# Decoder layer on one core: the last two turns reordered, and the closing layer norm laid out 32 tokens in a row per partition

## The chip, the cores and the metric

One NeuronCore of a Trainium2 chip runs one program. Times are device microseconds (us) of that core. TensorE is called PE here, VectorE DVE, ScalarE ACT, GpSimd POOL and SyncE SP, as in the profile's rows.

## What is computed

A post-norm decoder layer on x of 16 sequences by 256 tokens by 512 features (N = 4096 tokens), all in float32:

```
x = _layernorm(x + _L0_attn_ref(x, ...))             # grouped-query attention, 16 heads of 32, rope
x = _layernorm(x + _L0_xattn_ref(x, ctx, ctx, ...))  # mLSTM: gated decay, per-head norm of h
x = _layernorm(x + _L0_ffn_ref(x, ...))              # top-2 of 16 experts + one shared expert
```

Inside the mLSTM each head's output is normed: `hn = (h - mu) * rsqrt(var + EPS)`. The feed-forward part routes each token to two of 16 experts (`silu(flat @ Wu[e]) * (flat @ Wg[e])) @ Wd[e]`) and adds a shared expert that all tokens pass.

## The kernel before, in words

The program has three blocks, one after the other, on all five engines.

**Turns** (`attention_and_mlstm`). The 16 sequences go through a software pipeline. A turn handles attention of sequence `b`, the mLSTM of `y = b - 1`, and router plus shared expert of `w = b - 2`. There are 18 turns; the last two are short: turn (None, 15, 14), in which no attention is left, and turn (None, None, 15), in which only routing and the shared expert of the last sequence are left. Each engine has its own instruction stream, written out by hand in `body` (SP, POOL, ACT, PE) and `front`/`back` (DVE); engines meet at semaphores (`sig`, `wait`). An engine runs its stream in order, so what stands behind a waiting instruction waits too.

The names that the change touches:

- `hvar`: 128 tokens by 2 x 16 heads, the variance of each head's output plus a floor. DVE writes it in `spread` (L909, L910, signal `hvar_done`). POOL takes it to the power -1/2 (L527, `hrstd_done`), and DVE multiplies the heads by it (L1065), then scales, adds and takes the second layer norm (L1067 to L1074), and writes `x2` (L1088, `x2_done`). PE's next turn starts with the transposes of `x2` (L1160).
- `down(t)`: the second matrix product of the shared expert (PE, L1414, two halves of 8 instructions each, signal `sd_ready`). DVE adds `x2` of the sequence before to it and gets `base` (L1079), before it overwrites `x2`.
- `ug(c)`: the first product of the shared expert, four chunks, each `su` (8 instructions) and then `sg` (8), L1205; ACT takes a tanh of it, and DVE makes `hT` from it in `hidden(c)` (L888, L893). `ug(c)` waits for `hidden(c - 2)`.
- `rank`: for the tokens of a sequence, the number of earlier tokens that chose each expert (PE, L1180 and L1181), from the one-hot choice that DVE makes (L959 to L971). DVE reads it (L767) and computes each token's row (`place_rows`), the shares, and in the last turn `first_tables` (L836 to L857), which ends with a small diagonal matrix.
- PE spreads that matrix over all partitions (L1249, `across_ready`), and DVE's `last_tables` (L863 to L882) makes the tables that steer the experts: `idx` first, then counts, slots and turns.
- With `idx` POOL fetches the first four lists of rows (`fetch_pairs`, L1448) and then gathers rows of `x2` (L1533).

**Experts** (`experts`). 79 tiles of 128 routed rows: PE transposes a gathered tile (L1647), multiplies (L1659), transposes (L1669) and multiplies again (L1678); POOL adds the scaled result to `sum_rows` in DRAM (L1548). PE starts this block once the last `base` is made.

**Finish** (`finish`). SP loads `sum_rows` in 8 groups of 1024 KB (L1733), DVE takes mean and variance (L1770, L1773), ACT applies them (L1748), and SP stores each group (L1736). Group g holds 4 tiles of 128 tokens; in a tile, partition p holds one token:

```
sum_v = sum_dram[0:N, :].rearrange("(t p) d -> p t d", p=P)
out_v = out.rearrange("b (t p) d -> p (b t) d", p=P)
```

So a partition's part of a group is four pieces of 2 KB from four places in DRAM.

## Time and profile before

| what | value |
|---|---|
| median of 3 runs | 2074.43 us (2070.18 to 2075.65) |
| the profiled execution, its own time | 2060.83 us |
| its span in the profile | 2059.3 us |
| granted clock of PE, mean over the span | 0.949 |
| busy share PE / DVE / ACT / POOL | 90% / 53% / 32% / 33% |
| start of turn (None, None, 15) on PE | 1497.7 us |
| start of the experts' first product | 1535.0 us |
| start of the finish block's loads | 2013.3 us |

The span is read from the first to the last instruction of the profiled execution; its own time lies 1.5 us above the span, and 13.6 us under the median of the three runs. Times in the rows below are from the start of the span. A timeline row gives start, duration, engine, line, operation, what is written and read, the count, and in brackets how long the engine sat idle before and what ended that. PEclk is the granted clock of PE: 1.00 is 2.4 GHz, 0.50 is 1.2 GHz.

### The profile page before, as it was taken

What the parts mean: (1) busy time and instruction counts of PE and PEld (TensorE: products, weight loads), DVE (VectorE), ACT (ScalarE), POOL (GpSimd) and SP (SyncE); (2) the same over time, 40 slices, a digit from 0 to 9 for tenths busy, and PEclk for the clock granted to TensorE, in tenths of its full rate; (3) what the DMA queues carried; (4) which work ended last, traced back from release to release, by engine and by line L of the source; (5) the groups of instructions that cost most, each with busy time, mean ns of one, the idle gap of its engine ahead of it and who ended that gap; (6) DMA issues with size and microseconds to landing.
All of it is one profiled execution on the core that took longest, in us unless ns stands there. A gap on an engine that the chain in (4) does not pass through costs nothing.

```text
span 2059.3 us, 35236 instructions
## 1 busy us (share of the span) xinstructions
PE 1847.0 (90%) x10928; PEld 1164.1 (57%) x10929; DVE 1101.3 (53%) x2408; ACT 649.0 (32%) x1371; POOL 689.3 (33%) x753
## 2 busy tenths in 40 slices
PE   5789999899999989899999989998779999999990
PEld 3457575666657566565756656575544444444440
DVE  3366675666667566666756666665442222222225
ACT  0243342424334252433424243332302212221224
POOL 3223233242322424132232423233133444444440
PEclk7889999999999999999999999999989999999995
DMA  5744244433524444242434334232324666656549
GB/s 159 206 87 110 69 94 106 96 101 61 120 65 97 112 90 105 56 120 63 99 94 106 99 65 120 62 80 67 110 97 99 128 168 164 151 120 146 90 74 336
DMA packets 151804, 225.94 MB, mean 110 GB/s; under 512 B 32272, under 2 KB 107024, under 8 KB 149200
## 3 DMA queue, kind: packets, MB, share of 16 engines
q1 hardware_dynamic: 101856, 132.41, 25.3%
q0 software_dynamic: 38112, 91.86, 19.8%
q10 hardware_dynamic: 11792, 1.13, 0.5%
q8 instruction: 22, 0.36, 0.1%
q14 instruction: 22, 0.18, 0.0%
HBM read 94.44 MB, written 48.57 MB: 69 GB/s over the span
## 4 chain that ended last, share of the span: by engine, by line
PE 77%; DVE 10%; issue 4%; ACT 3%; DMA 2%; another core or an unknown queue 1%; SPq 1%; POOL 1%; DVEq 0%; ACTq 0%; POOLq 0%
PE ps L1659 13%; PE ps L1205 10%; PE ps L1137 8%; PE ps L1678 7%; PE ps L1439 5%; PE ps L1414 5%; PE ps L1298 4%; PE ps L1403 4%; PE ps L1334 3%; PE ps L1281 3%; DVE smax L917 3%; DVE arden L935 2%; PE ps L1152 2%; PE ps L1383 2%; PE ps L1260 2%
## 5 line engine op out<-in xcount | busy, mean ns | idle before, releaser
L1659 PE MATMUL ps<-ug_w,rowsT 128*128 x632 | 289.2, 601 | 7.9 <-SPq L1508 4.5
L1659 PEld LDWEIGHTS ps<-ug_w,rowsT 128*128 128x128 f32 x632 | 121.3, 193 | 162.0 <-issue 162.0
L1548 POOL DMA_INDIRECT sum_rows<-y_sb,pairs x79 | 125.7, 1591 | 245.6 <-DVE y_sb L1626 126.9
L511 POOL DMA_INDIRECT routed_ids<-pair_w,pos_w x64 | 64.0, 999 | 428.0 <-DVE pair_w L813 413.4
L935 DVE RECIPROCAL arden<-ps 128x256 f32<-128x256 f32 x64 | 112.5, 1758 | 177.1 <-PE ps L1403 174.2
L1137 PE MATMUL ps<-wqkv_sb,xT_sb 128*128 128x256 f32 (+1 forms) x512 | 174.7, 495 | 5.9 <-DMA wqkv_sb<-in_wqkv 5.9
L1030 DVE SCALAR_TENSOR_TENSOR weighted<-ps,decay 128x384 f32<-128x384 f32 x256 | 140.4, 554 | 61.9 <-PE ps L1281 53.5
L917 DVE TENSOR_REDUCE smax<-ps 128x2 f32<-128x512 f32 x256 | 163.8, 682 | 15.3 <-PE ps L1334 15.3
L1614 DVE SCALAR_TENSOR_TENSOR silu<-tanh,ps 128x256 f32<-128x256 f32 x79 | 33.3, 421 | 249.5 <-ACT tanh L1569 249.5
L668 ACT ACTIVATE decay<-ps,g_col 128x256 f32<-128x256 f32 x256 | 121.3, 474 | 139.9 <-PE ps L1262 103.0
L689 ACT ACTIVATE probs<-ps 128x1024 f32<-128x1024 f32 x128 | 125.8, 1022 | 80.9 <-PE ps L1383 80.9
L1678 PE MATMUL ps<-d_w,hidT 128*128 x316 | 148.6, 593 | 0.1
L1569 ACT ACTIVATE tanh<-ps 128x256 f32<-128x256 f32 x79 | 30.3, 384 | 370.9 <-PE ps L1659 361.6
L1137 PEld LDWEIGHTS ps<-wqkv_sb,xT_sb 128*128 128x128 f32 x512 | 96.8, 192 | 86.9 <-issue 79.4
L1334 PE MATMUL ps<-k_stack,q_stack 96*128 96x256 f32 x512 | 113.8, 327 | 30.6 <-DMA q_stack<-qkT_hi 12.9
L575 ACT COPY hid_sq<-ps 128x320 f32<-128x320 f32 x32 | 13.6, 425 | 397.0 <-PE ps L1137 397.0
L527 POOL TENSOR_TENSOR hvar<-hvar,eps_half 128x32 f32<-128x32 f32 x16 | 87.4, 5465 | 149.7 <-DVE hvar L910 149.7
L1205 PE MATMUL ps<-x2T,su_sb 128*128 128x256 f32 x512 | 125.5, 389 | 3.8 <-DVE hT L893 3.8
L1205 PE MATMUL ps<-x2T,sg_sb 128*128 128x256 f32 x512 | 121.6, 380 | 0.0
L1383 PE MATMUL ps<-q_stack,k_stack 98*128 98x256 f32 x512 | 92.0, 322 | 32.1 <-ACT probs L689 19.1
L1439 PE MATMUL ps<-wo_sb,hid_sq 128*128 128x512 f32 x256 | 114.3, 600 | 5.5 <-DVE hid_sq L937 5.5
L1298 PE MATMUL ps<-weighted,ctx_sb 128*32 128x256 f32 (+1 forms) x1024 | 109.4, 335 | 6.0 <-issue 5.3
(258 smaller groups left out, 3585.2 us busy)
## 6 DMA issues: line engine op xcount, KB each, us to landing
q_stack<-qkT_hi SPq DMA_DIRECT2D x128, 128.0 KB, 5.0
mk_stack<-ctxT_hi SPq DMA_DIRECT2D x128, 128.0 KB
mq_stack<-qkT_hi SPq DMA_DIRECT2D x128, 128.0 KB, 2.5
ug_w<-in_expert_ug SPq DMA_DIRECT2D x16, 1024.0 KB, 5.6
xT_sb<-in_xT SPq DMA_DIRECT2D x16, 512.0 KB, 3.3
x_sb<-in_x POOLq DMA_DIRECT2D x16, 512.0 KB, 3.8
ctxT_sb<-in_ctxT POOLq DMA_DIRECT2D x16, 512.0 KB, 4.6
ctx_sb<-in_ctx_in POOLq DMA_DIRECT2D x16, 512.0 KB, 8.1
```

The lines of the kernel that those rows point to most:

```text
L689: nc.scalar.activation(probs[:, i % 4, :, :, :].rearrange("p j t s -> p (j t s)"), ps[:, 2 * (i % 2):2 * (i % 2) + 2, :].rearrange("p j n ...
L917: nc.vector.tensor_reduce(smax[:, k, :], ps[:, 3 + 4 * (k % 2), :].rearrange("p (t s) -> p t s", s=S), AX.X, ALU.max).then_inc(smax_done.s ...
L935: nc.vector.reciprocal(arden[:, :], ps[:, 6 + c % 2, cols]).then_inc(arden_done.sem, 1)
L1030: nc.vector.scalar_tensor_tensor(weighted[:, h % 4, :], ps[:, qk2_bank(h), 0:384], SCALE, decay[:, h % 2, :], ALU.mult, ALU.mult).then_inc ...
L1137: ins = nc.tensor.matmul(ps[:, 2 * t + lo // 512, 0:hi - lo], xT_sb[:, c, P * t:P * t + P], wqkv_sb[:, c, lo:hi], start=c == 0, stop=c == ...
L1205: ins = nc.tensor.matmul(ps[:, 6 + c % 2, lo:lo + S], wt[:, k, P * c:P * c + P], x2T[:, k, :], start=k == 0, stop=k == KC - 1)
L1298: nc.tensor.matmul(ps[lo:lo + HD, 4 + i // 4, col + cols.start:col + cols.stop], ctx_sb[:, t, h, :], weighted[:, h % 4, part], start=t == ...
L1334: ins = nc.tensor.matmul(ps[:, 3 + 4 * (k % 2), S * t:S * t + S], q_stack[0:96, k, P * t:P * t + P], k_stack[0:96, k // GQ, :], start=True ...
L1383: ins = nc.tensor.matmul(ps[:, 2 * (i % 2) + j, S * t:S * t + S], k_stack[0:98, h // GQ, P * t:P * t + P], q_stack[0:98, h, :], start=True ...
L1439: ins = nc.tensor.matmul(ps[:, 6 + t, :], attT[:, c, P * t:P * t + P], wo_sb[:, c, :], start=c == 0, stop=c == KC - 1)
L1659: ins = nc.tensor.matmul(ps[:, 2 + k % 2, :], rowsT[:, k % 2, c, :], ug_w[:, bass.ds(slot, 1), c, :].rearrange("p o n -> p (o n)"), start= ...
L1678: ins = nc.tensor.matmul(ps[:, 4 + k % 2, :], hidT[:, k % 2, f, :], d_w[:, bass.ds(slot, 1), f, :].rearrange("p o d -> p (o d)"), start=f ...
```

## The change

Five edits; the first four act in the last two turns alone.

1. In turn (None, 15, 14) the power -1/2 on POOL is replaced by a square root on ACT (behind `square`) and a reciprocal on DVE. All other turns keep POOL's.
2. In the same turn both halves of `down` also wait for `hvar_done`.
3. In the last turn `rank` stands between the `su` and the `sg` half of `ug(0)`, not behind `ug(0)`, and the spreading of the diagonal matrix stands ahead of `ug(3)`, not behind it.
4. In the last turn `last_tables` stands ahead of `hidden(2)`, not behind `hidden(3)`.
5. In `finish`, partition p holds tokens 32p to 32p + 31, so that its part of a group is one piece of 8 KB, in `sum_rows` and in the output alike.

A signal is renamed too (`ln1_step` to `norm_step`), as the reciprocal steps it once more at the end.

```
                 if y is not None:
-                    wait(pool, hvar_done, y, 1)
-                    nc.gpsimd.tensor_tensor(hvar[:, :], hvar[:, :], eps_half[:, :], ALU.pow).then_inc(hrstd_done.sem, 1)
+                    if b is not None:
+                        wait(pool, hvar_done, y, 1)
+                        nc.gpsimd.tensor_tensor(hvar[:, :], hvar[:, :], eps_half[:, :], ALU.pow).then_inc(hrstd_done.sem, 1)
...
                         square()
+                        wait(act, hvar_done, y, 1)
+                        nc.scalar.activation(hvar[:, :], hvar[:, :], ACT.Sqrt).then_inc(hrstd_done.sem, 1)
...
                         nc.vector.tensor_tensor(g_log, g_cumf, g_max, ALU.add).then_inc(g_cols.sem, 1)
+                    if last:
+                        last_tables()
                     if w is not None:
                         hidden(2)
...
                         hidden(3)
-                    if last:
-                        last_tables()
...
                         wait(dve, hrstd_done, y, 1)
+                        if b is None:
+                            nc.vector.reciprocal(hvar[:, :], hvar[:, :]).then_inc(norm_step.sem, 1)
+                            wait(dve, norm_step, y + 1, 1)
                         wait(dve, hid_done, y, 2)
...
                             ins = nc.tensor.matmul(ps[:, 6 + c % 2, lo:lo + S], wt[:, k, P * c:P * c + P], x2T[:, k, :],
                                                    start=k == 0, stop=k == KC - 1)
+                        if c == 0 and lo == 0 and b is None and y is None:
+                            rank(ps[:, 0, 0:2 * ST * E])
...
-                    if b is None and y is None:
-                        rank(ps[:, 0, 0:2 * ST * E])
                     for c in range(1, SC):
                         if y is not None and c == 2:
                             rank(ranks_of_turn)
+                        if c == SC - 1 and b is None and y is None:
+                            pe.wait_ge(diag_done.sem, 3)
+                            nc.tensor.matmul(ps[:, 1, 0:3 * P], ones_k[:, 0:1].to_broadcast([P, P]), sq_flat[:, 0:3 * P],
+                                             start=True, stop=True).then_inc(across_ready.sem, 1)
                         ug(c)
-                    if b is None and y is None:
-                        pe.wait_ge(diag_done.sem, 3)
-                        nc.tensor.matmul(ps[:, 1, 0:3 * P], ones_k[:, 0:1].to_broadcast([P, P]), sq_flat[:, 0:3 * P],
-                                         start=True, stop=True).then_inc(across_ready.sem, 1)
...
                     elif y is not None:
                         wait(pe, decay_done, y, H)
+                        wait(pe, hvar_done, y, 1)
...
-        sum_v = sum_dram[0:N, :].rearrange("(t p) d -> p t d", p=P)
-        out_v = out.rearrange("b (t p) d -> p (b t) d", p=P)
+        sum_v = sum_dram[0:N, :].rearrange("(p t) d -> p t d", p=P)
+        out_v = out.rearrange("b s d -> (b s) d").rearrange("(p t) d -> p t d", p=P)
```

PE in the last turn, before (after the routing product L1173; `su_sb` and `sg_sb` are the two halves of `ug`, L1180 and L1181 the ranks, L1249 the spreading, L1414 `down`):

```order
L1205 MATMUL ps<-x2T,su_sb 128x256 x4
L1205 MATMUL ps<-x2T,sg_sb 128x256 x4
L1180 MATMUL ps<-biased,before_sb 128x32
L1181 MATMUL ps<-biased,ones_k 128x32
L1205 MATMUL ps<-x2T,su_sb 128x256 x4
L1205 MATMUL ps<-x2T,sg_sb 128x256 x4
L1205 MATMUL ps<-x2T,su_sb 128x256 x4
L1205 MATMUL ps<-x2T,sg_sb 128x256 x4
L1205 MATMUL ps<-x2T,su_sb 128x256 x4
L1205 MATMUL ps<-x2T,sg_sb 128x256 x4
L1249 MATMUL ps<-hid_sq,ones_k 128x384
L1414 MATMUL ps<-sd_sb,hT 128x512 x8
```

The same place in the changed kernel (its lines stand a few numbers later):

```order
L1211 MATMUL ps<-x2T,su_sb 128x256 x4
L1186 MATMUL ps<-biased,before_sb 128x32
L1187 MATMUL ps<-biased,ones_k 128x32
L1211 MATMUL ps<-x2T,sg_sb 128x256 x4
L1211 MATMUL ps<-x2T,su_sb 128x256 x4
L1211 MATMUL ps<-x2T,sg_sb 128x256 x4
L1211 MATMUL ps<-x2T,su_sb 128x256 x4
L1211 MATMUL ps<-x2T,sg_sb 128x256 x4
L1254 MATMUL ps<-hid_sq,ones_k 128x384
L1211 MATMUL ps<-x2T,su_sb 128x256 x4
L1211 MATMUL ps<-x2T,sg_sb 128x256 x4
L1421 MATMUL ps<-sd_sb,hT 128x512 x8
```

The ranks moved up by one half of `ug(0)`, the spreading by all of `ug(3)`; the count of instructions is the same. (The order's listing counts a float32 matmul once; the profile shows it as two.)

ACT at the end of turn (None, 15, 14) and the start of the last, in the changed kernel (L640 copies the heads' output, L645 is `square`, L590 and L600 belong to the last turn, L583 is its first tanh):

```order
L640 COPY hid_sq<-ps 128x2x256 [waits x2_done,num_ready]
L645 ACTIVATE weighted<-hid_sq 128x1024 [waits av2_pair,hid_done]
L686 ACT_TABLE_LOAD
L686 ACTIVATE hvar<-hvar 128x32 [waits hvar_done]
L590 COPY x2T<-ps 128x1024 [waits num_ready,x2T_ready]
L600 COPY arden<-ps 128x256 [waits lgT_ready]
L583 ACT_TABLE_LOAD [waits silu_done]
L583 ACTIVATE gate_sb<-ps 128x256 [waits ug_ready]
```

The two table loads and the square root (L686) are new; the load of L686 waits for no signal, and the square root waits for `hvar_done`.

## Rows read from the trace of the kernel before

**Rows 1.** The page, section 4: shares of the chain that ended last, by engine.
```profile
PE 77%; DVE 10%; issue 4%; ACT 3%; DMA 2%; another core or an unknown queue 1%; SPq 1%; POOL 1%; DVEq 0%; ACTq 0%; POOLq 0%
```
**Rows 2.** Timeline, DVE, end of turn (None, 15, 14).
```profile
1484.00 0.19 DVE L910 SCALAR_TENSOR_TENSOR hvar<-hvar,mrden 128x32 f32<-128x32 f32 x1
1489.78 1.22 DVE L1065 TENSOR_TENSOR hid_sq<-hid_sq,hvar 128x1024 f32<-128x1024 f32 x1 [5.59 <-POOL hvar L527]
...
1494.97 1.27 DVE L1079 TENSOR_TENSOR base<-ps,x 128x512 f32<-128x512 f32 x2
1496.38 1.22 DVE L1088 TENSOR_SCALAR x<-hid_sq,mv,rstd 128x512 f32<-128x512 f32 x2
```
**Rows 3.** Timeline, PE, same stretch.
```profile
1480.06 0.44 PE L1319 MATMUL ps<-id_sb,denT 128*128 128x128 f32 x2 [2.32 <-ACT denT L679]
...
1480.77 7.03 PE L1414 MATMUL ps<-sd_sb,hT 128*128 128x512 f32 x16
1497.66 1.97 PE L1160 MATMUL ps<-id_sb,x 128*128 128x128 f32 x8 [9.85 <-DVE x L1088]
```
**Rows 4.** Timeline, ACT, an earlier table load and the square of this turn.
```profile
1443.43 1.28 ACT L609 ACT_TABLE_LOAD   x1
...
1481.59 1.06 ACT L644 ACTIVATE weighted<-hid_sq 128x1024 f32<-128x1024 f32 x1
```
**Rows 5.** Windows: start:end, length, busy us of PE, PEld, DVE, ACT, POOL, PEclk, DMA share, GB/s.
```profile
1445.90:1447.80 1.90, 0.00 (x0) 0.00 (x0) 0.84 (x3) 1.28 (x3) 0.00 (x0) 1.00 0.93 195
1448.60:1452.00 3.40, 3.40 (x9) 2.66 (x8) 2.49 (x6) 0.00 (x0) 0.00 (x0) 0.50 0.00 0
...
1493.00:1506.50 13.50, 7.25 (x28) 5.35 (x29) 6.31 (x21) 1.38 (x2) 2.54 (x4) 0.50 0.57 228
```
**Rows 6.** Timeline, DVE, the last turn.
```profile
1503.37 0.19 DVE L959 COPY logits<-ps 128x32 f32<-128x32 f32 x1 [5.77 <-PE ps L1173]
...
1505.34 0.19 DVE L971 TENSOR_TENSOR biased<-onehot 128x32 f32<-128x32 f32 x1
1508.96 0.22 DVE L767 COPY hid_sq<-ps 128x64 f32<-128x64 f32 x1 [3.43 <-PE ps L1181]
...
1516.19 0.78 DVE L857 TENSOR_SCALAR hid_sq<-id_sb,hid_sq 128x128 f32<-128x128 f32 x3
...
1522.78 0.55 DVE L863 COPY hid_sq<-ps 128x384 f32<-128x384 f32 x1
...
1525.56 0.19 DVE L882 TENSOR_SCALAR turns<-hid_sq 1x79 int32<-1x79 f32 x1
...
1530.09 0.69 DVE L1079 TENSOR_TENSOR base<-ps,x 128x512 f32<-128x512 f32 x1 [2.74 <-issue]
```
**Rows 7.** Timeline, PE, the last turn and the experts' first tile.
```profile
1512.34 1.99 PE L1205 MATMUL ps<-x2T,su_sb 128*128 128x256 f32 x8
...
1521.37 0.81 PE L1249 MATMUL ps<-hid_sq,ones_k 128*128 128x384 f32 x2
1522.92 7.13 PE L1414 MATMUL ps<-sd_sb,hT 128*128 128x512 f32 x16 [0.74 <-DVE hT L893]
1532.50 0.63 PE L1647 MATMUL ps<-id_sb,rows 128*128 128x128 f32 x4 [2.44 <-DMA rows<-x_rows,pairs]
1535.00 6.53 PE L1659 MATMUL ps<-ug_w,rowsT 128*128 x8 [1.87 <-issue]
```
**Rows 8.** Time to landing of the loads L1733 and the stores L1736.
```profile
DMA to landing us min/median/max: 5.7/12.9/14.8
...
DMA to landing us min/median/max: 5.3/8.3/12.2
```
**Rows 9.** Landing of the expert weights' loads L1503; windows with 8 KB and with 2 KB pieces.
```profile
DMA to landing us min/median/max: 5.1/5.6/9.8
...
1488.00:1492.90 4.90, 0.00 (x0) 0.00 (x0) 3.05 (x3) 0.00 (x0) 1.74 (x1) 1.00 1.00 417
2016.00:2053.00 37.00, 0.00 (x0) 0.00 (x0) 26.27 (x88) 23.67 (x40) 0.00 (x0) 0.50 1.04 395
```

More of the change, by code:

```diff
@@ L281, in attention_and_mlstm @@
         wo_ready, h_done = sig("wo_ready", ST), sig("h_done", ST)
-        ln1_step, mv1_done, rstd1_step, rstd1_done = sig("ln1_step", ST), sig("mv1_done", ST), sig("rstd1_step", 1), sig("rstd1_done", 1)
+        norm_step, mv1_done, rstd1_step, rstd1_done = sig("norm_step", ST), sig("mv1_done", ST), sig("rstd1_step", 1), sig("rstd1_done", 1)
         x1_done = sig("x1_done", ST)
@@ L1096, in back @@
                             wait(dve, h_done, b, t + 1)
-                            nc.vector.bn_stats(stats1[:, t, :], x1[:, t, :]).then_inc(ln1_step.sem, 1)
+                            nc.vector.bn_stats(stats1[:, t, :], x1[:, t, :]).then_inc(norm_step.sem, 1)
                         for t in range(ST):
-                            wait(dve, ln1_step, b, t + 1, rest=rest)
+                            wait(dve, norm_step, b, t + 1, rest=rest)
                             nc.vector.bn_aggr(mv1[:, t, :], stats1[:, t, :]).then_inc(mv1_done.sem, 1)
```

## The prediction

> **What bounds the kernel now.** I first read the chain of waits: 77% of it is PE, 10% DVE [rows 1]. In the sixteen full turns and in the experts PE is nearly always busy, and the change leaves both alone. It works where PE is not the bound: from the end of turn (None, 15, 14) to the experts' first product, and in the finish block. So I took the timelines of DVE, PE and ACT there, then windows for PE's granted clock, then the DMA of the finish.
>
> End of turn (None, 15, 14): DVE has the variance at 1484.19, then sits idle for 5.59 us behind POOL's power, and writes x2 from 1496.38 to 1497.60 [rows 2]. PE has done both halves of down long before (1480.77 to 1487.80) and idles 9.85 us [rows 3]. This chain alone sets the start of the last turn.
>
> Last turn: let T be the start of the logits' copy, 1503.37. The choice is made at T + 2.2, but the ranks are read at T + 5.6, since they stand behind both halves of ug(0) on PE. The diagonal matrix is done at T + 13.6, 8.0 after the ranks; the tables are begun at T + 19.4 and take 3.0; the last base is made at T + 27.4 [rows 6]. PE begins the last down at T + 19.55, ends it at T + 26.7, and the first gathered rows come at T + 29.1, 1.7 after the last base; the first expert product starts at T + 31.6 [rows 6, 7].
>
> PE's clock: granted 0.50 from 1493.0 to 1506.5, after PE had done nothing since 1487.8 [rows 3, 5]. The experts' first product takes 6.53 us for 8 instructions [rows 7], where half as much is usual at the full clock.
>
> Finish: 16 transfers of 1024 KB are 16.8 MB. From 2016 to 2053 the DMA engines are busy all the time and move 395 GB/s [rows 9], and the last store lands 5.3 us after its issue [rows 8].
>
> **The root (edit 1).** Off the path: 5.59 us of DVE's idle time [rows 2]. On it come a square root on ACT and a reciprocal on DVE, 128 by 32 each. Neither is in the trace at this shape; the lower bound is DVE's 0.19 for the same shape [rows 2], the upper ACT's 1.06 for 32 times the elements [rows 4]. I take 0.2 each, the shape being the same, plus 0.2 for the hand-overs: 0.6. The table load costs 1.28 us [rows 4]; it waits for no signal, so it starts behind the square, at 1482.65, and is over at 1483.93, 0.26 before the variance. The load back for the tanh lies behind the copy of the logits' parts, where ACT waits for PE's ug(0): nothing. If that cover were gone it would be 1.28. So DVE's chain is **5.0 sooner** up to the norm's statistics, from about 1495.0 to 1490.0.
>
> **down held back (edit 2).** PE now starts down at about 1484.3, not 1480.8. At the full clock its 7.03 us end at 1491.3. The second half of base, which started at about 1495.6, needs that end plus 0.2; base and x2 follow, and x2 starts at 1492.3, so of the 5.0 only 4.1 are left. Moreover PE now does nothing from 1477.7 to 1484.3 except 0.7 us of transposes [rows 3]. The trace shows what less than that did: PE idle for 1.9 us ahead of 1447.8, and then 3.4 us at half the clock [rows 5]. In 3.4 us at half clock PE does 1.7 us of work less, so down ends at 1493.0 and x2 comes **2.4 sooner**. That is my value; bounds are 4.1 (no such stretch) and 0.7 (a stretch twice as long).
>
> **The clock after it.** Before, the first 13.5 us of the stretch from 1493.0 on have 7.25 us of PE work at half clock [rows 5], 3.6 at full; some 2 of the difference lie on the way to T. In the changed kernel PE's hole ahead of x2 shrinks from 9.85 to about 2 us, so the clock may stay up, but as the 1.9 us hole shows it need not. Between 0 and 2, I take **0.5**, near the lower end, since there the nearest row is the 1.9 us one.
>
> **Ranks and tables sooner (edits 3 and 4).** From T at full clock: choice at T + 2.2, ranks (0.8 with hand-over) read at T + 3.0, sg done at T + 4.9, diagonal matrix at T + 11.0. PE does ug(1) and ug(2), each 2 halves of 1.8 to 2.0 [rows 7], until T + 12.2, then the spreading (0.8) until T + 13.0. DVE's tables take 3.0, until T + 16.0; hidden(2) and hidden(3), now behind them, need 0.9 each and 0.4 for the tanh between: down starts at T + 18.2, not 19.55. The rows to be gathered are asked for some 6 us sooner and are no longer waited for; PE now goes on with the last base, T + 26.1, and needs about 2.6 from there (transposes, ACT's issue of two DMAs ahead of its copy, and the 1.87 of loads of registers [rows 7]): first product at T + 28.7 in place of 31.6. I take **2.8**; bounds 1.3 (only down's start moves) and 3.5.
>
> **The first product's clock.** PE's pause ahead of it falls from 2.44 + 1.87 to about 0.9 + 1.9. If the clock stays up, 6.53 becomes 3.3 [rows 7]. Between 0 and 3.2; I take **0.5**, as a pause of nearly 2 us remains.
>
> **Long rows in the finish (edit 5).** The nearest stretch with 8 KB pieces is the expert weights', with 4 KB ones among them: 417 GB/s at a DMA share of 1.00 [rows 9]. 16.8 MB take 42.5 us at 395 and 40.2 at 417: 2.2 less. But DVE and ACT need their own 30 us between first landing and last store; by the ends alone the first load could land at 5.1 instead of 5.7 and the last store at 5.1 instead of 5.3 [rows 8, 9], 0.8 in all. I take **1.6** between these two. Issue on SP is hidden behind DVE.
>
> The Trainium skill speaks against this part: its page "DMA: Bandwidth & Descriptors", section Specifications, has pieces of 512 B and more at line rate, so that 2 KB would be as good as 8 KB. By that rule the sum would be 1.6 smaller. The trace has 395 against 417 GB/s, so I keep my value.
>
> **Sum.** 2.4 + 0.5 + 2.8 + 0.5 + 1.6 = 7.8 us. The profiled execution took 2060.8, so I expect 2053.0 for it; against the median of the runs, 13.6 us higher, **2066.6**. About 0.3%, 6.2 us, is what a measurement of this kernel can tell from no change: the border is 2068.2.
>
> **Rivals.**
> - **The clock stays up.** PE's holes are all about 2 us or less but one, and several holes of that kind in the turns cost nothing. Then x2 gains 4.1, the way to T 2.0, the last turn 2.8, the first product 2.8, the finish 2.2: 13.9, 2060.5. Against it: the stretch after 1447.8 [rows 5].
> - **The held down gives back what the root gave.** Half clock lasts through nearly all of down; x2 gains 0.7, PE idles at the same places as before, the finish gives 0.8: with 2.8 for the tables 4.3, 2070.1. For it: the hole of 6.6 us with 0.7 of work in it is much longer than the 1.9 us that sufficed. Against it: down itself is 7 us of unbroken work, and 1448.6 to 1452.0 was short.
> - **Rows do not matter in the finish**, all else as forecast: 6.2, 2068.2, just on the border, counted as the same.
> - **The finish becomes slower.** All 128 partitions now read and write at a distance of 64 KB from one another, where a group was one closed piece of 1 MB. The turns and tables give 6.2, so the kernel is slower by 0.3% if the finish loses 12.4: 42.5 us become 55, at about 305 GB/s. If it ran at the 228 GB/s of [rows 5], as one example of a slow stretch, it would take 74 us, 31 more: 2099. Nothing in the trace shows such a pattern; the weights with 8 KB pieces lie close together.
>
> The Trainium skill knows such an effect, in the same page, section "Latency and other measured facts": distances between partitions' rows that are large powers of two slow the copies, but at 512 KiB it still has nearly the full rate. 64 KB is far below; no run here shows it yet.
>
> **Chances.** Forecast 0.52 (its own range 2063.5 to 2069.5, seven eighths of it under the border), clock stays up 0.15, given back 0.20, rows do not matter 0.08, slower finish 0.05. Faster by over 0.3%: 0.52 x 7/8 + 0.15 = 0.61. Slower 0.05, the rest, 0.34, the same. The range reaches from the second case to a little over the third: 2060 to 2072.
>
> **What would show it.** In the changed profile DVE's idle time ahead of the product with hvar falls to about 0.6; ACT shows a table load that ends before the variance; down starts at the variance. Whether PEclk is 0.50 within down decides between 2.4 and 4.1. T lies about 3 us sooner; ranks are read 3.0 after T; the experts' first transposes no longer wait for the gathered rows. In the finish the rate is above 410 GB/s, or the last part is wrong. I am wrong on the whole if x2 isn't sooner, or if the finish takes longer from its first load to the end than 46 us.

## The result, and the profile after

| | before | changed |
|---|---|---|
| median | 2074.61 us (22 runs, 2068.14 to 2077.86) | 2065.86 us (22 runs, 2056.83 to 2076.89) |
| the profiled execution, its own time | 2060.83 us | 2056.83 us |
| its span | 2059.3 us | 2055.3 us |
| granted clock of PE, mean | 0.949 | 0.951 |

The ratio of the times is 0.9962, 95% interval 0.9952 to 0.9972: 7.9 us faster (5.8 to 10.0), by more than the 0.3% that I called measurable, though the interval reaches a little below it. The medians themselves are 8.75 us apart. The forecast was 7.8 us less than the earlier median of three runs, 2066.6. One execution of the kernel before in the first batch of the experiments below took 3065 us at a mean clock of 0.554, and the ratios leave it out.

The two profiled executions differ by only 4.0 us. Both are unusually fast: the one before (2060.83) lies below the lowest of its 22 runs, and the changed one is the lowest of its own. The page shows nothing of where the difference comes from: the chain is PE 77% before [rows 1], and now

```profile
PE 78%; DVE 10%; ACT 4%; issue 3%; another core or an unknown queue 2%; DMA 1%; SPq 1%; DVEq 0%; ACTq 0%; POOLq 0%
```

So I cut each trace at places that both kernels have: the variance (end of L910, now L913), the start of x2 (L1088, now L1094), the logits' copy T (L959, now L962), the start of the first expert product (L1659, now L1666), its end, and the first load of the finish. Lengths in us:

| stage | before | changed |
|---|---|---|
| start of the span to the variance | 1484.2 | 1492.5 |
| variance to the start of x2 | 12.19 | 10.30 |
| x2 to T | 6.99 | 5.25 |
| T to the first expert product | 31.63 | 27.53 |
| that product (8 instructions) | 6.53 | 3.70 |
| its end to the finish's first load | 471.8 | 471.7 |
| finish, from its first load's issue to the end | 46.0 | 44.2 |

The last six are 12.3 us shorter. The first is 8.35 longer, in the sixteen full turns and the start, whose code is the same in both; that is how much executions of one program differ, and why a stage, not a span, is compared below. In the same way 12.3 is not the gain of a typical execution, as the experiments will show.

**The root.** DVE and ACT at the variance, changed kernel (timeline; compare [rows 2, 4]):

```profile
1491.01 1.28 ACT L686 ACT_TABLE_LOAD   x1
...
1492.35 0.19 DVE L913 SCALAR_TENSOR_TENSOR hvar<-hvar,mrden 128x32 f32<-128x32 f32 x1
1492.57 0.23 ACT L686 ACTIVATE hvar<-hvar 128x32 f32<-128x32 f32 x1 [0.28 <-DVE hvar L913]
1492.68 9.29 PE L1421 MATMUL ps<-sd_sb,hT 128*128 128x512 f32 x16 [3.78 <-DVE hvar L913]
1492.83 0.35 DVE L1068 RECIPROCAL hvar<-hvar 128x32 f32<-128x32 f32 x1 [0.29 <-ACT hvar L686]
1493.22 1.23 DVE L1071 TENSOR_TENSOR hid_sq<-hid_sq,hvar 128x1024 f32<-128x1024 f32 x1
```

The table load ends 0.28 us before the root starts, the root takes 0.23 and the reciprocal 0.35. From the variance's end (1492.54) to the product with hvar there are 0.68 us, where there were 5.59.

**down held back.** DVE gets the halves of down late (changed kernel, timeline), and the clock is half in a part of them (windows; columns as in [rows 5]):

```profile
1498.58 0.69 DVE L1085 TENSOR_TENSOR base<-ps,x 128x512 f32<-128x512 f32 x1
...
1502.01 0.69 DVE L1085 TENSOR_TENSOR base<-ps,x 128x512 f32<-128x512 f32 x1 [2.74 <-PE ps L1421]
1502.84 1.22 DVE L1094 TENSOR_SCALAR x<-hid_sq,mv,rstd 128x512 f32<-128x512 f32 x2
```
```profile
1488.90:1492.60 3.70, 0.01 (x1) 0.00 (x0) 1.89 (x5) 2.96 (x4) 0.00 (x0) 0.68 0.64 184
1492.60:1496.80 4.20, 4.12 (x5) 1.83 (x6) 3.87 (x4) 0.20 (x1) 0.00 (x0) 0.50 1.08 422
1496.80:1502.00 5.20, 5.17 (x12) 1.91 (x10) 2.36 (x6) 0.00 (x0) 0.95 (x2) 0.97 0.95 394
1502.00:1504.00 2.00, 0.00 (x0) 0.00 (x0) 1.85 (x3) 0.00 (x0) 0.83 (x1) 1.00 1.03 422
1504.00:1509.00 5.00, 3.30 (x25) 2.48 (x26) 0.86 (x7) 2.67 (x3) 0.76 (x1) 1.00 0.94 381
```

PE idles from 1488.9, its granted clock is 0.68 on average over that idle stretch and 0.50 in the first 4.2 us of down; down takes 9.29 us, not 7.03. DVE waits 2.74 us for it. In exchange the hole (PE's idle stretch) ahead of x2 is short, about 2.1 us, and the last turn begins at the full clock, where before it was half until 1506.5 [rows 5].

**Ranks and tables** (changed kernel, timeline of DVE, then of PE; compare [rows 6, 7]). T is 1508.09:

```profile
1508.09 0.19 DVE L962 COPY logits<-ps 128x32 f32<-128x32 f32 x1 [4.04 <-PE ps L1179]
...
1510.97 0.23 DVE L770 COPY hid_sq<-ps 128x64 f32<-128x64 f32 x1 [0.72 <-PE ps L1187]
...
1518.20 0.68 DVE L860 TENSOR_SCALAR hid_sq<-id_sb,hid_sq 128x128 f32<-128x128 f32 x3
...
1520.34 0.56 DVE L866 COPY hid_sq<-ps 128x384 f32<-128x384 f32 x1 [0.67 <-issue]
...
1522.82 0.19 DVE L885 TENSOR_SCALAR turns<-hid_sq 1x79 int32<-1x79 f32 x1
...
1532.31 0.69 DVE L1085 TENSOR_TENSOR base<-ps,x 128x512 f32<-128x512 f32 x1 [2.74 <-PE ps L1421]
```
```profile
1519.49 0.81 PE L1254 MATMUL ps<-hid_sq,ones_k 128*128 128x384 f32 x2
...
1525.13 7.13 PE L1421 MATMUL ps<-sd_sb,hT 128*128 128x512 f32 x16 [1.38 <-DVE hT L896]
1533.10 0.63 PE L1654 MATMUL ps<-id_sb,rows 128*128 128x128 f32 x4 [0.83 <-DVE base L1085]
1535.62 3.69 PE L1666 MATMUL ps<-ug_w,rowsT 128*128 x8 [1.90 <-ACT rowsT L1589]
```

Ranks are read at T + 2.9, the diagonal matrix is done at T + 10.8, the tables at T + 14.9, down starts at T + 17.0, the last base ends at T + 24.9, and the transposes follow base and no longer the gathered rows.

**Finish** (changed kernel: SP's issues, landing of the loads and of the stores, one window; compare [rows 8, 9]):

```profile
2011.04 4.04 SPq L1740 DMA_DIRECT2D ctotal<-sum_rows  x8
2025.69 25.04 SPq L1743 DMA_DIRECT2D out_rows<-ctotal  x8
```
```profile
DMA to landing us min/median/max: 4.8/11.8/20.6
...
DMA to landing us min/median/max: 4.5/7.8/12.0
```
```profile
2013.70:2050.70 37.00, 0.00 (x0) 0.00 (x0) 26.28 (x88) 24.19 (x40) 0.00 (x0) 0.50 1.00 411
```

411 GB/s in place of 395. SP issued the eight loads in 4.04 us; in the kernel before it took

```profile
2013.29 12.84 SPq L1733 DMA_DIRECT2D ctotal<-sum_rows  x8
```

The gain of the finish lies at its two ends. DVE's first instruction stands 4.8 us behind the first load's issue (before: 5.7), and the end of the kernel 4.9 us behind the last store's issue (before: 5.7). The time from the one to the other is 34.5 us in the changed kernel and 34.6 in the kernel before. In it DVE and ACT go from group to group, and DVE waits for a load only once, for the first. A few microseconds ahead of the last store's issue the DMA engines are still busy all the time in the kernel before, while in the changed kernel their share falls to 0.83 for 2 us (windows, the kernel before first):

```profile
2049.30:2053.30 4.00, 0.00 (x0) 0.00 (x0) 0.00 (x0) 4.00 (x7) 0.00 (x0) 0.50 1.05 408
```
```profile
2047.00:2049.00 2.00, 0.00 (x0) 0.00 (x0) 0.00 (x0) 2.00 (x4) 0.00 (x0) 0.50 0.83 348
```

### The profile page after: what moved, and what is told of

It reads as the page before. It is cut to its first block, busy times and chain, and to the rows that moved or that the text cites. A ratio compares the mean times of both kernels' runs of the same rounds, so it can differ in the third digit from the quotient of the medians.

```text
span 2055.3 us, 35239 instructions
## 1 busy us (share of the span) xinstructions
PE 1843.0 (90%) x10928; PEld 1163.2 (57%) x10929; DVE 1101.7 (54%) x2409; ACT 651.7 (32%) x1374; POOL 684.6 (33%) x752
## 4 chain that ended last, share of the span: by engine, by line
PE 78%; DVE 10%; ACT 4%; issue 3%; another core or an unknown queue 2%; DMA 1%; SPq 1%; DVEq 0%; ACTq 0%; POOLq 0%
PE ps L1666 13%; PE ps L1211 11%; PE ps L1143 8%; PE ps L1685 7%; PE ps L1421 6%; PE ps L1446 5%; PE ps L1409 4%; PE ps L1304 4%; PE ps L1340 3%; PE ps L1287 3%; DVE arden L938 3%; DVE smax L920 3%; PE ps L1158 2%; PE ps L1266 2%
## 5 line engine op out<-in xcount | busy, mean ns | idle before, releaser
L1666 PE MATMUL ps<-ug_w,rowsT 128*128 x632 | 286.3, 596 | 8.0 <-SPq L1515 4.6
L1666 PEld LDWEIGHTS ps<-ug_w,rowsT 128*128 128x128 f32 x632 | 120.2, 191 | 160.3 <-issue 160.2
L528 POOL TENSOR_TENSOR hvar<-hvar,eps_half 128x32 f32<-128x32 f32 x15 | 82.0, 5468 | 157.4 <-DVE hvar L913 157.4
L1421 PE MATMUL ps<-sd_sb,hT 128*128 128x512 f32 x256 | 116.3, 608 | 5.2 <-DVE hvar L913 3.8
```

The lines of the kernel that those rows point to most:

```text
L1421: ins = nc.tensor.matmul(ps[:, 2 + t, :], hT[:, c, P * t:P * t + P], sd_sb[:, c, :], start=c == 0, stop=c == SC - 1)
L1666: ins = nc.tensor.matmul(ps[:, 2 + k % 2, :], rowsT[:, k % 2, c, :], ug_w[:, bass.ds(slot, 1), c, :].rearrange("p o n -> p (o n)"), start= ...
```

## The experiments

The eleven runs came in three batches, on three chips. There the kernel before takes 1997 us (medians 1996.92, 1997.78 and 1997.26), where it took 2075 above; the record doesn't name the chip of the first pair, and I take it to be another. Nearly all of the difference lies ahead of the variance (1416 to 1423 us in place of 1484 and 1493). The stages behind it are about as long as above, but the stretch from the first expert product's end to the finish's first load, 471.8 and 471.7 us above, ranges from 471.4 to 474.2 us in the eleven profiles. The half-held version below has 474.0 in one execution and 471.4 in another, so even this stage moves by more than some of the gains looked for. Ratios are against the kernel before in the same batch. At the end of the section one table has the stages of all of them.

### Down not held back

```
-                        wait(pe, hvar_done, y, 1)
```

> The changed kernel without edit 2: both halves of down run again right behind the transposes, under the root. Theory (the hold costs what it takes from the root): from the variance to the start of x2 7.2 us, where the changed kernel's profile has 10.3 and the kernel before 12.2; PE then idles some 5 us ahead of x2 and its clock may fall there, so that from x2 to the logits' copy it is 5.3 to 7.0. In all 1 to 3 us faster than the changed kernel, ratio to the kernel before 0.9945 to 0.9957. Rival (the hold pays, because it keeps the clock up for the last turn): the half clock behind x2 takes 3 us or more, and the kernel is slower than the changed one, 0.9965 or above.

1987.23 us, ratio 0.9947 (0.9932 to 0.9961). x2 starts 7.29 after the variance, where 7.2 was expected, and then the way to T is 6.98. The ratio is within the range of the theory. All of the root's gain reaches x2, and PE has its hole again (timeline, PE; windows):

```profile
1429.18 1.11 PE L1166 MATMUL ps<-id_sb,x 128*128 128x128 f32 x4 [4.95 <-DVE x L1094]
```
```profile
1424.20:1429.00 4.80, 0.04 (x1) 0.00 (x0) 4.63 (x9) 0.00 (x0) 1.78 (x3) 0.76 1.02 369
1429.00:1431.00 2.00, 1.82 (x8) 1.57 (x8) 0.13 (x1) 0.00 (x0) 0.76 (x1) 0.50 0.97 401
1431.00:1434.90 3.90, 2.31 (x14) 1.28 (x14) 0.00 (x1) 2.50 (x3) 0.00 (x0) 0.50 1.02 426
1434.90:1439.90 5.00, 5.00 (x14) 4.17 (x15) 2.52 (x17) 0.17 (x1) 0.00 (x0) 0.50 0.52 211
```

The clock falls in the hole and is half for the 10.9 us from 1429.0 to 1439.9. So the two orders place one slow stretch differently: ahead of x2, or behind it.

### Pieces of 2 KB in the finish, as before

```
-        sum_v = sum_dram[0:N, :].rearrange("(p t) d -> p t d", p=P)
-        out_v = out.rearrange("b s d -> (b s) d").rearrange("(p t) d -> p t d", p=P)
+        sum_v = sum_dram[0:N, :].rearrange("(t p) d -> p t d", p=P)
+        out_v = out.rearrange("b (t p) d -> p (b t) d", p=P)
```

> The changed kernel without edit 5: four pieces of 2 KB per partition and group again. Theory (long rows move more bytes a second): the finish, from its first load's issue to the end, takes 46.0 us as before and not 44.3, first load landing 5.7 and last store 5.3 where the changed kernel has 4.8 and 4.5; ratio 0.997. Rival (the finish was sooner by chance, or because it began in a quieter moment): 44.3 us and 0.9962 again.

1991.4 us, 0.9973 (0.996 to 0.9986). The finish is 45.92 us again, with all else changed; its loads land after 5.6/12.9/14.9 us and the rate is

```profile
1950.00:1985.00 35.00, 0.00 (x0) 0.00 (x0) 26.26 (x88) 24.19 (x40) 0.00 (x0) 0.50 1.05 398
```

By the finish's length the long pieces are worth 1.7 us. That is edit 5 by itself, as forecast: the finish takes 45.6 to 46.0 us in the three profiles with 2 KB pieces and 43.8 to 44.6 in the ten with 8 KB. The ratio alone couldn't tell it (0.9973 here, 0.9965 and 0.9962 for the changed kernel, with overlapping intervals). Edit 5 changes two things at once, the length of a piece and the distance between the partitions' rows, and no run separates them. The code from the variance to the experts is here the changed kernel's word for word, and yet that way took 51.4 us up to the end of the first product, not 46.8: x2 to T 5.88, T to the product 29.22, the product itself 6.76. The clock goes with it. It is still 1.00 over the hole of 2.1 us ahead of x2's transposes, then 0.77 up to 1436.9, 0.54 in the 5.1 us after that, and 0.54 again in the product, where the changed kernel's profile has 1.00 in all of them.

### Ranks and tables late, as before

Edits 3 and 4 undone, all else changed:

```
-                        if c == 0 and lo == 0 and b is None and y is None:
-                            rank(ps[:, 0, 0:2 * ST * E])
...
+                    if b is None and y is None:
+                        rank(ps[:, 0, 0:2 * ST * E])
                     for c in range(1, SC):
...
-                    if last:
-                        last_tables()
                     if w is not None:
                         hidden(2)
...
                         hidden(3)
+                    if last:
+                        last_tables()
```

> The changed kernel without edits 3 and 4: ranks behind ug(0), spreading behind ug(3), last tables behind hidden(3). Theory: from the logits' copy to the experts' first product 31 to 31.6 us as before, where the changed kernel has 27.5; 4 us slower than the changed kernel, and up to 3 more where PE's clock falls in the longer pause ahead of the first product; ratio 0.9980 to 0.9995. Rival (down's start alone moved, the rest is the clock's): 28.8 us and less than 2 us slower.

1992.71 us, 0.9974 (0.9959 to 0.9989), under the 0.9980 to 0.9995 that was expected. Down starts 20.4 after T, the first product 32.5, and PE waits for the gathered rows again:

```profile
1465.91 0.63 PE L1654 MATMUL ps<-id_sb,rows 128*128 128x128 f32 x4 [2.33 <-DMA rows<-x_rows,pairs]
```

That is 4.9 more than 27.53, but here the clock was half for 5 us after T (0.50). Against the two profiles with the new order and the clock down in the same place (29.22 and 29.43) it is 3.0 to 3.3 more. By the ratio, edits 3 and 4 are worth about 2 us (0.9974 against 0.9965), which is not clear of the noise.

### The root on POOL, down not held

Edits 1 and 2 undone:

```
-                        wait(pe, hvar_done, y, 1)
...
-                        nc.scalar.activation(hvar[:, :], hvar[:, :], ACT.Sqrt).then_inc(hrstd_done.sem, 1)
...
-                            nc.vector.reciprocal(hvar[:, :], hvar[:, :]).then_inc(norm_step.sem, 1)
...
+                    wait(pool, hvar_done, y, 1)
+                    nc.gpsimd.tensor_tensor(hvar[:, :], hvar[:, :], eps_half[:, :], ALU.pow).then_inc(hrstd_done.sem, 1)
```

> The changed kernel without edits 1 and 2 (POOL's power again, down at once): tables sooner and long rows alone. Theory (edits 1 and 2 together are worth 2 to 4 us): from the variance to x2 12.2 us, to the logits' copy another 7.0 at half clock; ratio 0.9970 to 0.9985. Rival (the root with the hold is worth nothing over all executions): 0.9962.

1991.96 us, 0.9975 (0.9964 to 0.9985). DVE waits again:

```profile
1423.74 1.22 DVE L1065 TENSOR_TENSOR hid_sq<-hid_sq,hvar 128x1024 f32<-128x1024 f32 x1 [5.58 <-POOL hvar L527]
```

x2 starts 12.19 after the variance, and T to the product is 29.66: with the root as before, the earlier tables alone bring 2.0 of the 31.63. Against the first experiment, which differs from this one by the root alone, x2 is 4.90 later, and the time 4.7 longer (1991.96 and 1987.23; by the means of 10 and 5 executions 4.9, give or take 2.8). So the root's gain is seen in the stage and in the time alike.

### The changed kernel again, on one of these chips

No edit.

> The changed kernel itself, on the chip of the four runs before. Of the four parts each undone run bounds one: without edit 5 it had 0.9973, without edits 3 and 4 0.9974, with the held down taken back 0.9947. Theory (the held down costs more than it brings): 0.9955 to 0.9965 here, so slower than with down not held; x2 starts 10.3 us after the variance against 7.3, the way from the variance to the end of the first expert product is 47 to 52 us depending on whether PE's clock falls in the last turn. Rival (the held down pays by the clock after it): ratio 0.9940 or less, and the way to the first product's end is under 49.1, the value with down not held.

1990.06 us, 0.9965 (0.9949 to 0.9981). The profiled execution was one with the clock up in the last turn: T to the product 27.53, the product 3.70, to the hundredth as in the first profile; x2 starts 9.81 after the variance, not 10.30. So its stages speak for the rival, as they are shorter than with down not held (46.3 against 49.1 from the variance to the product's end), and its ratio for the theory (0.9965 against 0.9947, intervals overlapping). Both together, below, settles it.

### Only the second half of down held, until the product with hvar is made

```
                         wait(pe, decay_done, y, H)
-                        wait(pe, hvar_done, y, 1)
+                        if t == 1:
+                            wait(pe, tail_step, y, 5)
```

> The changed kernel, but the first half of down starts at once, and the second half waits until DVE has made the product with the reciprocal. Theory: PE's one hole ahead of x2 is then cut in two, of about 2 and 3 us, x2 starts as early after the variance as with down not held (7.3 us), and the last turn starts with the clock up in more executions: from x2 to the logits' copy 5.3 to 6 us instead of 7.0. Ratio 0.9935 to 0.9947. Rival (the clock falls with two holes of this size as with one): 7.3 and 7.0 us as with down not held, ratio 0.9947.

1984.97 us, 0.9933 (0.9918 to 0.9949). Timeline of PE, and windows:

```profile
1417.31 3.60 PE L1422 MATMUL ps<-sd_sb,hT 128*128 128x512 f32 x8
...
1422.78 3.67 PE L1422 MATMUL ps<-sd_sb,hT 128*128 128x512 f32 x8 [1.87 <-DVE hid_sq L1071]
...
1429.28 1.09 PE L1166 MATMUL ps<-id_sb,x 128*128 128x128 f32 x8 [2.83 <-DVE x L1094]
```
```profile
1426.50:1429.20 2.70, 0.00 (x0) 0.00 (x0) 2.56 (x6) 0.00 (x0) 1.78 (x3) 1.00 1.00 350
1429.20:1434.00 4.80, 3.12 (x21) 2.01 (x21) 0.03 (x1) 2.37 (x3) 0.76 (x1) 0.65 1.01 398
1434.00:1440.00 6.00, 6.00 (x23) 5.05 (x23) 3.59 (x23) 0.45 (x2) 0.00 (x0) 0.71 0.74 306
```

x2 is as early as with down not held, neither half of down is slowed, and the clock falls later and for less: 6.11 from x2 to T, in place of 6.98 (5.3 to 6 was expected). One hole of 4.95 has become two of 1.87 and 2.83. Of this kernel and the changed one in the same batch the medians are 5.1 us apart.

### Other ends of the finish

The first load in two halves, each with a signal of its own; the last group normalised by DVE itself. Two waits of SP that cost no time are added for the halves.

```
+            sp.dma_start(total[:, 0:G // 2, :], sum_v[:, 0:G // 2, :]).then_inc(out_sem, 16)
+            sp.dma_start(total[:, G // 2:G, :], sum_v[:, G // 2:G, :]).then_inc(total_in[0], 16)
...
+            dve.wait_ge(shift_done, NT // G)
+            for n in range(NT - G, NT):
+                v.tensor_scalar(total[:, n, :], total[:, n, :], rstd[:, n:n + 1], shift[:, n:n + 1],
+                                ALU.mult, ALU.add).then_inc(own_step, 1)
```

> The changed kernel with other ends of the finish: the first load is cut in two halves with a signal each, and DVE normalises the last group itself. With the DMA at its rate all the time, the finish is 16.8 MB at about 411 GB/s, 40.9 us, plus the first load's flight and the last store's. Theory (rows and ends set the finish, the middle is at the DMA's rate): 44.2 becomes 41.5 to 43 us, ratio 0.001 lower than the changed kernel's in the same batch. Rival (the middle absorbs it: the last load's landing sets the last store, not the first landing): under 0.5 us, no difference in the ratio.

1990.43 us, 0.9964 (0.995 to 0.9977), against 0.9965 for the changed kernel: nothing. From the first load's issue the finish takes 43.8 us, where it took 44.2; the other profiles with 8 KB pieces have 43.9 to 44.6, so this is no clear gain either. The theory fell. The rival was right in size but not in its reason, since the last store is issued much sooner: DVE begins 3.9 us after the first issue, in place of 4.8, and the last store is issued 36.3 us after it (1982.8 - 1946.5), in place of 39.2 (1981.5 - 1942.3). But from there it takes 7.4 us to the end of the kernel, where the changed kernel's took 5.0. This kernel, timelines of DVE and SP, its stores by their source line, and a window:

```profile
1950.40 2.67 DVE L1786 BATCH_NORM_STATS2 cstats<-ctotal 128x6 f32<-128x512 f32 x4 [10.69 <-DMA ctotal<-sum_rows]
```
```profile
1946.51 0.33 SPq L1739 DMA_DIRECT2D ctotal<-sum_rows  x1
...
1982.38 0.81 SPq L1751 DMA_DIRECT2D out_rows<-ctotal  x2
```
```profile
L1751 SPq DMA_DIRECT2D out_rows<-ctotal x8: 332/333/382, 1960.5 to 1982.8; - x8
```
```profile
1950.00:1987.00 37.00, 0.00 (x0) 0.00 (x0) 28.32 (x92) 21.38 (x36) 0.00 (x0) 0.50 1.01 421
```

What the ends gain is waited for in the queue of the DMA engines, whose share is 1.01 in this window and 1.02 from 1982.8 to 1986.5, after the last store's issue: 16.8 MB at 411 to 421 GB/s are 40 to 41 of the 44 us. So two limits lie within half a microsecond of one another in the changed kernel: the groups' way through DVE and ACT, and the DMA's rate. Relieving the first alone brings nothing.

### Both together

The diffs of the first experiment and of the one just above.

> Down not held, and the finish's ends as in the run before: a version meant to beat the changed kernel. Theory: the two gains add up, 0.9947 less 0.001, so 0.9937, about 4 us faster than the changed kernel. Rival (the held down was not what cost): no better than the run before.

1986.93 us, 0.9944 (0.9928 to 0.9961), where the theory had 0.9937. This is down not held over again (0.9947), and nothing for the ends. It also answers the question of the held down. In this batch all of down was held in 17 executions (the changed kernel again, and the one with other ends), mean 1990.0 us, and not held in 6, mean 1986.5: 3.5 us less, give or take 2.9. The pair that differs by edit 2 alone, both with other ends, gives 3.9, give or take 3.1. So edit 2 costs more than it brings.

### The hole filled

Behind an unheld down, six products of the same shape into a PSUM bank that nobody reads:

```
+                    if b is None and y is not None:
+                        for i in range(6):
+                            nc.tensor.matmul(ps[:, 0, :], hT[:, i % SC, 0:P], sd_sb[:, i % SC, :], start=True, stop=True)
```

> The changed kernel with down not held, and behind down six products of the same shape whose result nobody reads (0.88 us each, 5.3 us): PE's hole of 6.1 us between the end of down and x2 shrinks to under 1 us. Theory (PE's clock falls behind that hole, and this is what the last turn loses): x2 at 7.3 us after the variance, from x2 to the logits' copy 5.3 instead of 7.0, to the first product's start 27.5 instead of 29.7, that product 3.7 instead of 5.2, together 5.5 us less than with down not held; ratio 0.9925. Rival (the clock falls for other reasons than PE's idle time there): 7.0 and 29.7 as with down not held, ratio 0.9947.

1985.76 us, 0.9939 (0.9922 to 0.9956). PE's timeline and windows:

```profile
1424.32 5.31 PE L1441 MATMUL ps<-sd_sb,hT 128*128 128x512 f32 x12
1429.47 1.04 PE L1166 MATMUL ps<-id_sb,x 128*128 128x128 f32 x8
```
```profile
1424.30:1429.50 5.20, 5.20 (x14) 2.17 (x13) 4.90 (x9) 0.00 (x0) 1.78 (x3) 1.00 0.98 302
...
1461.00:1466.00 5.00, 5.00 (x8) 2.11 (x9) 0.00 (x0) 0.00 (x0) 0.94 (x1) 0.66 0.44 138
```

Three of the four numbers of the theory came: x2 at 7.28, then 5.25, then 27.54. The clock is full from down to the last base:

```profile
1424.30:1458.00 33.70, 29.88 (x119) 19.33 (x117) 19.81 (x86) 4.37 (x8) 13.63 (x16) 1.00 0.49 177
```

The fourth number did not come: the first product takes 5.39, not 3.70, at 0.66. The ratio, 0.9939, is also less of a gain than the 0.9925 of the theory, and its interval takes in the rival's 0.9947; it is the stages that decide for the theory.

### The kernel before with the hole filled

The same lines with `range(10)` in the kernel before, nothing else.

> The kernel before, with ten such products behind down (8.8 us of the hole of 9.85), all else as it was: the price of the clock by itself. Theory: from x2 to the logits' copy 5.3 instead of 7.0, to the first product's start 29.5 to 30 instead of 31.6, and that product 5.2 to 6.5; ratio 0.9975 to 0.9985. Rival: nothing moves, ratio 1.000.

1993.31 us, 0.9981 (0.9968 to 0.9993). x2 to T 5.25 (6.99), T to the product 29.77 (31.63), x2 12.19 after the variance as ever, all as the theory had it. The clock from T to the product:

```profile
1433.80:1463.60 29.80, 23.19 (x91) 15.96 (x90) 15.54 (x78) 2.32 (x6) 11.68 (x12) 1.00 0.18 56
```

With the clock full throughout, then, the way from T is 29.77 in the old order and 27.53 in the new: the earlier ranks and tables by themselves bring **2.2**, and the clock of the last turn 1.7 + 1.9 = 3.6 in a profile in which it stays up.

### The half-held version again

No edit against the version above.

> The version with only the second half of down held, once more, beside the filled one. Theory: 0.9933 again within 0.001, some 2 us slower than the filled one, since the first product of the last turn still runs at half the clock. Rival (0.9933 was luck of that batch): 0.9947 or above, as with down not held.

1986.51 us, 0.9946 (0.9928 to 0.9964), nearer to the rival. The stages up to the product's end repeat to 0.15 us; the first product is 3.70 again, so the half clock that the theory put there was not there. 0.9933 was in part luck of its batch; against the filled version (0.9939) and against down not held (0.9947, 0.9944) no difference can be told.

### All stages

| kernel | variance to x2 | x2 to T | T to product | product | sum | finish | ratio |
|---|---|---|---|---|---|---|---|
| before | 12.19 | 6.99 | 31.63 | 6.53 | 57.3 | 46.0 | 1 |
| changed, first pair | 10.30 | 5.25 | 27.53 | 3.70 | 46.8 | 44.2 | 0.9962 |
| changed, again | 9.81 | 5.25 | 27.53 | 3.70 | 46.3 | 44.2 | 0.9965 |
| pieces of 2 KB | 9.57 | 5.88 | 29.22 | 6.76 | 51.4 | 45.9 | 0.9973 |
| other ends | 9.77 | 5.67 | 29.43 | 5.16 | 50.0 | 43.8 | 0.9964 |
| tables late | 9.72 | 5.72 | 32.47 | 5.29 | 53.2 | 44.6 | 0.9974 |
| down not held | 7.29 | 6.98 | 29.61 | 5.26 | 49.1 | 43.9 | 0.9947 |
| not held, other ends | 7.29 | 6.98 | 29.83 | 5.15 | 49.2 | 44.2 | 0.9944 |
| root on POOL, not held | 12.19 | 6.98 | 29.66 | 6.69 | 55.5 | 44.1 | 0.9975 |
| half held | 7.28 | 6.11 | 28.57 | 3.69 | 45.7 | 44.4 | 0.9933 |
| half held, again | 7.29 | 6.11 | 28.71 | 3.70 | 45.8 | 44.4 | 0.9946 |
| hole filled | 7.28 | 5.25 | 27.54 | 5.39 | 45.5 | 44.4 | 0.9939 |
| before, hole filled | 12.19 | 5.25 | 29.77 | 5.39 | 52.6 | 45.6 | 0.9981 |

Four profiles have the changed kernel's code from the variance to the first product's end, and of these two had the clock up afterwards (46.3 and 46.8) and two had not (50.0 and 51.4); their mean, 48.6, is 8.7 under the 57.3 of before. With the finish's 1.8 that is 10.5, against one profile of the kernel before. The ratio says 7.9; the experts' stage between the two, which moves by up to 2.8 us, is left out of this sum.

**A version faster than the changed kernel.** Half held: 0.9933 and 0.9946, against 0.9965, 0.9964 and 0.9962 wherever all of down was held until the variance and the finish had long pieces. The means of the two and of the three differ by 0.0024, 4.8 us. Taken as independent, with half widths of 0.0010 to 0.0018 each, that difference is known to about 0.0014, so it is a gain; and the trace has a reason for 2.5 to 3 us of it, at x2. Against simply leaving edit 2 out, though, no gain of the half-held version is shown: in their common batch the means are 1984.5 and 1986.5, 2.0 us apart, give or take 3.3. By the stages it is 3.4 us shorter (45.7 and 45.8 against 49.1 and 49.2). It does no work for nothing, unlike the filled one.

## Why the prediction was right, point by point

**The time** came out 0.7 us beside the forecast (2065.86, 2066.6), and within the range. By the time alone, the likeliest case was the one that happened; "clock stays up" (2060.5), "given back" (2070.1), "rows don't matter" and "finish slower" did not, though the first of them comes near the profiled execution of the changed kernel (12.3 against its 13.9) in all but x2, for which it had 4.1 and 1.9 came, since down did run at half clock.

**The root**: 5.0 forecast, 4.91 measured up to the product with hvar (5.59 to 0.68), and 4.90 at x2 once nothing else stands in the way. The table load was hidden, and the load back too. The Trainium skill's price is higher: its page "ScalarE: Activation LUTs", section "What ACT_TABLE_LOAD costs", adds a drain of 1.38 us to the load's 1.28. By that the root would have started about 1.1 us later; the row shows the root 0.28 us after the end of the load, and waiting for the variance alone. In the kernel before, too, an ACT load that ends at 1444.71 is followed by its first activation at 1444.72. The drain, if there was one, isn't on these paths.

**down held back**: forecast 2.4 of the 5.0 at x2; measured 1.9, 2.4, 2.4, 2.5 and 2.6 in five profiles. The mechanism is the one named: half clock in the first 3 to 4 us of down, and DVE waiting for its second half. What the forecast doesn't say is that edit 2 is a loss by its own terms: it put x2 at 2.6 us later than the root alone would allow, and gave the clock after it 0.5 and that of the first product 0.5. The runs have 3.5 us (give or take 2.9) in favour of no hold.

**The clock after it**: forecast 0.5, bounds 0 and 2. This term was too small. It is 1.7 in two profiles, and 1.1 to 1.3 in three; I had put it near the lower end by the one row of 1.9 us of idle time [rows 5], and the holes of 2.1 us here did not cost the clock in two of the five profiles. That the clock is what holding buys, and that the hole ahead of x2 is what costs it, is shown by the filled kernels: fill the hole, and 6.99 becomes 5.25 with nothing else changed.

**Ranks and tables sooner**: forecast 2.8 (28.7 from T). At the full clock it is 2.2, from 29.77 to 27.53; before against changed is 4.1 because 1.9 of the old 31.63 was the half clock [rows 5], which I had put into the other terms or not at all. Single steps: ranks 2.9 (3.0), matrix 10.8 (11.0), tables done 14.9 (16.0), down 17.0 (18.2), base 24.9 (26.1), product 27.5 (28.7). Nearly all of the miss of 1.2 arises before down starts: ug(1) and ug(2) begin at T + 4.5, not 4.9, and end at T + 11.4, not 12.2, since each half starts 1.73 us after the one before, where I had added durations of 1.8 to 2.0 [rows 7] that overlap; and the tables took 2.7, not 3.0.

**The first product's clock**: forecast 0.5, bounds 0 and 3.2. Measured 2.8, 2.8, 1.4 and -0.2 in the four profiles with the changed kernel's code. It was undersized in three of them, and it has the widest spread of all.

**Long rows**: forecast 1.6, measured 1.75 between the two profiles and 1.7 by the experiment. I took a value between the rate's 2.2 and the ends' 0.8, and this compromise rests on no row, so that it met the number is in part luck. Two readings fit what was measured. By the rate, 16.8 MB are 42.5 us at 395 and 40.9 at 411, 1.6 less. By the ends, the first load lands 0.9 sooner and the last store takes 0.8 less, 1.7 in all, twice the 0.8 that I had; between them stand 34.5 us of DVE and ACT, not the 30 of the forecast. The experiment with other ends shows that with 8 KB pieces the two limits nearly meet, so they aren't told apart. The Trainium skill's page "DMA: Bandwidth & Descriptors", section Specifications, gives 512 B as the least transfer at line rate. Read as I read it, that 2 KB pieces would be as fast as 8 KB ones, it doesn't hold in these numbers: 395 and 398 GB/s against 411, with the DMA share at 1.00 or above in each. The same page of the Trainium skill, section "Latency and other measured facts", has 207 of 214 GB/s at a row distance of 512 KiB and nothing for 64 KB; with rows 64 KB apart these runs moved 411 GB/s and more, so no slowdown shows.

**The sum.** 7.8 forecast. The terms of the changed kernel in a profile with the clock up are 1.9 + 1.7 + 4.1 + 2.8 + 1.75 = 12.3; the clock's terms were all too small for it. In the profile with the clock down again (that of the 2 KB pieces) they are 2.6 + 1.1 + 2.4 - 0.2 = 5.9, and with the finish's 1.75 it would be 7.7 in all. That 7.8 met the median is thus partly right terms and partly luck: it depends on how often the clock stays up, which nothing in the forecast gave, and the forecast of the single terms was less good than that of their sum. One slip in the chances: of the range 2063.5 to 2069.5 the part under the border of 2068.2 is 0.78 by length, not seven eighths, which would give 0.56 for "faster" in place of 0.61.

**What stays open.** First, where the held down loses its 3.5 us. By the stages it should gain a little (48.6 on average against 49.2), by the times it costs (ratios 0.9964 against 0.9946, and 3.5 us between the means of one batch). The profiles, of one execution each, don't show where those microseconds are. Second, why the first expert product takes 3.70 in four profiles, 5.2 to 5.4 in six, and 6.5 to 6.8 in three. The changed kernel and the filled one reach it with the same timing to 0.01 us, and still have 3.70 and 5.39. So it isn't the idle time just ahead of it alone.

## What to carry to other kernels

An idle stretch of PE can be paid twice, by the wait and then by half clock in what follows (here a hole of 4.95 us, and 1.7 us more from x2 to T than with the hole filled); price a move by where it puts the hole. Holding back all of the work that is ready moved the slow stretch ahead of x2 and cost 3.5 us; holding back half of it did not cost that, but is not shown to beat holding back nothing. Compare stages between places that both traces have: here executions of one program differed by 8 us ahead of the change, more than the change is worth. And where the DMA engines are busy nearly all the time, earlier starts and shorter ends brought nothing; longer pieces did.

## What the runs showed of the hardware

- One operation, x to the power -1/2 for 128 by 32 values, takes 5.47 us on POOL; a square root on ACT and a reciprocal on DVE take 0.23 and 0.35 with 0.1 for the hand-overs.
- SP's issue of eight loads of 1 MB took 12.84 us with 2 KB pieces and 4.04 with 8 KB ones. The first issue alone took 0.39 and 0.33 us, so most of the difference is in the later ones. It did not matter here, since DVE waited for no load but the first.
- The same program took 2075 us in one place and 1997 on three chips. In the profiles of before and changed, and of the eleven runs, the way up to the variance of the last but one turn is 1484 and 1493 us against 1416 to 1423. The experts (471.4 to 474.2 us) and the finish were about as long on all.
- Six products for nothing on an idle PE (5.3 us) delayed nothing (x2 at 7.28, as without them) and kept the clock at 1.00 for the 28.5 us that followed, up to the last base.
